# Loads and stores of a graph layer cut into 112 + 13 and 96 + 7 rows, lists issued by another engine, one drain fewer

## Chip, cores and metric

One core of a Trainium2 chip runs the whole program. The metric is the device time of one execution in microseconds. The time shown for a kernel is the median of its runs.

## The reference

One layer of a graph network on 3,125 nodes of 128 features and 53,125 edges of 64 features, all float32. The edges are sorted by their destination `dst`. Cut to what is computed:

```
h   = relu(bn(concat(x[src], edge_attr) @ W1 + b1, g1, be1))   # bn over all edges
s   = segment_sum(h, dst);  cnt = segment_sum(1, dst)
agg = where(cnt > 0, s / max(cnt, 1), 0)
h2  = relu(bn(concat(x, agg) @ W2 + b2, g2, be2))              # bn over all nodes
out = layernorm(x + relu(h2 @ Wl + bl))                        # per node
```

## The kernel before

It is written by hand against the engines: one block of instructions for each engine, ordered as written, with semaphores between them. SyncE (`sp`) issues most DMAs, ScalarE (`act`) some, GpSimd (`pool`) the gathers. A DMA adds 16 to its semaphore when it has landed. There are five stages.

**Start.** `x` lies as 125 partitions of 25 rows. It comes in four loads (`XLOADS`, line 413), is turned by TensorE (line 686, `turn_x`), copied by VectorE (line 992), multiplied by the upper part of W1 (line 702), copied by ScalarE (line 846) and stored as the table `ytab` in DRAM by four stores (`YSAVES`, line 429). W1 is first multiplied by the signs of g1 (lines 984 to 986). The lists `src` and `dst` are loaded as 104 groups of 512 edges, one group to a partition, by `load_lists` (lines 402 and 404): 103 full rows and the remainder in a transfer of its own. VectorE turns them into floats (lines 999, 1000) between its copies of batches 1 and 2, and TensorE spreads them before the last batch. GpSimd starts its gathers when the table has landed (`s_tab`) and the indices stand (`s_idx`).

**Edge loop.** 26 steps of four groups of 512 edges. GpSimd gathers table rows by four indirect DMAs a group (line 606), SyncE loads edge features (`load_ea`, line 435), TensorE turns and multiplies them (716, 722), VectorE adds and sums, ScalarE squares. Three groups of a step stay in SBUF in `res`; the fourth is spilled to DRAM (861). The one-hot matrices go to DRAM too (864), and the products of x with W2 (`h2x_dram`, 877). VectorE adds up the number of edges of each node in `cnt`.

**Spread phase.** 26 steps of four groups. SyncE loads the one-hot matrices back (`load_hot`, 474) and the spilled rows (`load_back`, 484); VectorE takes the maximum (1142), TensorE sums by node in windows of 64 nodes (778), ScalarE copies the window (915), and GpSimd adds it to `agg` (624). On the side the counts go to DRAM (325), VectorE inverts them (`invert_counts`), they go to DRAM once more (329), and from step 10 on they are spread to all partitions of `cnt` by `counts_back` (333), one transfer for every two steps and one for the rest (`last_counts_back`, 337). `load_nodes` (494, 498) and `load_rest` (506, 509) bring `h2x_dram` and x, the latter as 125 partitions of three rows.

**Seam.** When all 104 windows are added, GpSimd drains (line 640) and sets `sums_over`. VectorE (line 1164, two chunks) and GpSimd (line 645, five chunks) multiply `agg` by the reciprocal counts; both wait for `sums_over` and the last of the counts. Before that VectorE scales W2 (line 1158) once all node inputs are there.

**Node phase.** TensorE multiplies the chunks by W2 (822), VectorE adds the part of x (1173), batch statistics follow, then relu, the product with Wl (835), the sum with x and the layer norm; ScalarE writes the normalised rows (line 320). SyncE stores them in seven transfers of 125 partitions by up to four rows (line 569) and waits for them.

```
q.dma_start(cnt[:, bass.ds(k * RCP, RCP)], rc_dram[bass.ds(k * RCP, RCP)].partition_broadcast(P))
pool.wait_ge(agg_added, NG)
pool.drain().then_inc(sums_over, 1)
```

Of the kernel before, what the change touches and what calls it, by code (L numbers as in the profile page):

```python
# [28 lines left out]
I32 = mybir.dt.int32  # L29
# [4 lines left out]
P = 128  # L34
# [3 lines left out]
GROUP = TILES * P  # L38
U = 4
# [6 lines left out]
def gnn_kernel(nc, x, src, dst, ea, W1, b1, g1, be1, W2, b2, g2, be2, Wl, bl, out):  # L46
# [3 lines left out]
    NT = 25  # L50
# [30 lines left out]
    with ctx:  # L81
# [40 lines left out]
        RCP = (N - 1) // RCN // 8 * 8  # L122
        XTP = NT // RCN
        NODEIN = 16 * ((H2 + 1) * (RCN + 1) + 3 + 3 * H2)
        TAB = 16 * (len(YSAVES) + 1)
# [271 lines left out]
        def _(sp):  # L397
            def load_lists():

                sp.wait_ge(s_rowset, 1)  # L400
                for r, d in ((srow, src), (drow, dst)):
                    sp.dma_start(r[0:NG - 1, :].bitcast(I32),
                                  d[0:(NG - 1) * GROUP].rearrange("(g e) -> g e", e=GROUP)).then_inc(s_rows, 16)
                    sp.dma_start(r[NG - 1:NG, 0:LAST].bitcast(I32),  # L404
                                  d[(NG - 1) * GROUP:E].rearrange("(g e) -> g e", g=1)).then_inc(s_rows, 16)
# [16 lines left out]
            yv = ytab[0:N, :].rearrange("(p t) f -> p t f", t=NT)  # L422
# [16 lines left out]
            for q in range(U):  # L439
                load_ea(0, q)  # L440
# [50 lines left out]
            def load_nodes(k, half):  # L491
# [5 lines left out]
                if half == 1:  # L497
                    sp.dma_start(xnv2[:, bass.ds(k * XTP, XTP), :],
# [808 lines left out]
```

## Time and profile before

| | |
|---|---|
| three runs, median | 919.43 us (916.29 to 920.59) |
| the profiled execution | 916.23 us, its span 914.5 us |
| mean granted clock of TensorE | 0.622 |
| busy: TensorE / GpSimd / VectorE / ScalarE | 442.7 / 461.7 / 388.4 / 195.4 us |
| moved by DMA | 83.91 MB, 92 GB/s over the span |

The profile is one execution. Times in it count from the start of the span. A row of the timeline gives the start, the duration, the engine, the line of the kernel, the operation, the tile written and those read, and in brackets how long the engine had been idle and what ended that. SPq and ACTq are the queues that issue DMAs; their durations are those of issuing, not of moving. The DMA share is the mean busy share of the core's 16 DMA engines. No engine is busy for much over half of the span, so the stages have to be read one by one.

### The profile page before, as it was taken

The numbers are of one execution on the slowest core, as the hardware profiler recorded it, in microseconds if no ns is written. First come the engines' busy times: TensorE is split into PE (matmuls) and PEld (weight loads), VectorE is DVE, ScalarE is ACT, GpSimd is POOL, SyncE is SP. The second block draws the span as 40 slices with busy tenths as digits, with TensorE's granted clock in tenths as the row PEclk, the third lists the DMA queues.
The fourth block names the chain that finished last, engine by engine and source line by source line (L and its number), as shares of the span: only waits on it lengthen the run. The fifth ranks groups of instructions, "written<-read, shape, count | busy, mean of one in ns | idle before, by whom it ended". The sixth has DMA issues, their size and how long they took to land.

```text
span 914.5 us, 11316 instructions
## 1 busy us (share of the span) xinstructions
PE 442.7 (48%) x2195; PEld 338.7 (37%) x2195; DVE 388.4 (42%) x801; ACT 195.4 (21%) x517; POOL 461.7 (50%) x572
## 2 busy tenths in 40 slices
PE   1541553443354434335435434544443459998572
PEld 1520332322233322223323222333222239998442
DVE  1331344433334443333444333344333377776385
ACT  0110111111111111111111111111111125645264
POOL 2056655555665555566555556655555623322352
PEclk9955556555555655555655555565555559999777
DMA  1232322323232322233323232333222224777202
GB/s 65 87 92 63 95 87 71 89 80 83 80 93 78 98 71 79 84 80 94 87 71 89 77 86 80 92 89 89 72 78 86 80 92 130 212 224 207 87 1 71
DMA packets 65233, 83.91 MB, mean 92 GB/s; under 512 B 19159, under 2 KB 44168, under 8 KB 65217
## 3 DMA queue, kind: packets, MB, share of 16 engines
q1 hardware_dynamic: 40529, 39.49, 15.2%
q0 software_dynamic: 13312, 27.29, 11.9%
q10 hardware_dynamic: 11376, 16.97, 5.0%
q14 instruction: 12, 0.10, 0.0%
q8 instruction: 4, 0.07, 0.0%
HBM read 63.61 MB, written 20.08 MB: 92 GB/s over the span
## 4 chain that ended last, share of the span: by engine, by line
another core or an unknown queue 45%; PE 22%; issue 9%; DMA 7%; ACT 5%; DVE 4%; ACTq 3%; SPq 3%; POOLq 1%; POOL 0%; DVEq 0%
PE psH L722 12%; DMA res<-spill 4%; PE psH L778 3%; ACT work L854 2%; PE psC L778 2%; PE psT L716 2%; ACT work L868 2%; DMA res<-in_x 2%; SPq L404 2%; ACTq L864 1%; DMA hotb<-hot_dram 1%; PE psH L702 1%; ACTq L877 1%; POOLq L640 1%
## 5 line engine op out<-in xcount | busy, mean ns | idle before, releaser
L722 PE MATMUL psH<-w1e,work 128*128 128x256 f32 x416 | 207.0, 650 | 390.8 <-ACT work L854 284.6
L606 POOL DMA_INDIRECT res<-ytab,srci x312 | 298.9, 958 | 140.9 <-issue 94.8
L722 PEld LDWEIGHTS psH<-w1e,work 128*128 128x128 f32 x416 | 117.6, 312 | 447.4 <-ACT work L854 310.0
L606 POOL DMA_INDIRECT work<-ytab,srci x104 | 100.6, 968 | 193.4 <-DVE res L1044 155.2
L854 ACT ACTIVATE work<-psT 128x256 f32<-128x256 f32 x104 | 40.0, 384 | 571.0 <-remote 417.3
L1058 DVE TENSOR_TENSOR psX<-work,psX 128x512 f32<-128x512 f32 x104 | 72.2, 694 | 120.6 <-issue 60.6
L1044 DVE TENSOR_TENSOR work<-psH,work 128x512 f32<-128x512 f32 x26 | 18.0, 692 | 163.3 <-remote 131.5
L1044 DVE TENSOR_TENSOR res<-psH,res 128x512 f32 (+1 forms) x78 | 54.0, 692 | 69.8 <-PE psH L722 37.2
L1142 DVE TENSOR_TENSOR work<-res,psX 128x512 f32<-128x512 f32 x103 | 70.7, 688 | 28.3 <-PE psC L778 11.5
L716 PE MATMUL psT<-ident,work 128*128 128x128 f32 x208 | 64.7, 411 | 8.9 <-DMA work<-in_edge_attr 7.6
L624 POOL TENSOR_TENSOR agg<-agg,srci 128x64 f32 x104 | 32.2, 309 | 68.1 <-ACT srci L915 66.2
L1038 DVE TENSOR_TENSOR cnt<-cnt,psC 128x64 f32 x104 | 23.1, 222 | 83.3 <-remote 78.5
L778 PE MATMUL psH<-work 128*128 128x128 f32 (+1 forms) x416 | 52.7, 281 | 6.4 <-ACT srci L915 4.8
L732 PEld LDWEIGHTS psC<-hotb,onesb 128*128 128x128 bf16 x416 | 40.5, 137 | 38.2 <-issue 28.6
L1051 DVE TENSOR_TENSOR psS<-res,psS 128x512 f32<-128x512 f32 x78 | 53.8, 690 | 0.0
L778 PEld LDWEIGHTS psH<-work 128*128 128x128 f32 x416 | 50.1, 197 | 7.5 <-ACT srci L915 5.7
L868 ACT ACTIVATE work<-res 128x512 f32 (+1 forms) x78 | 49.0, 628 | 13.9 <-issue 11.2
L778 PE MATMUL psC<-work 128*128 128x128 f32 (+1 forms) x416 | 51.4, 277 | 0.0
L778 PEld LDWEIGHTS psC<-work 128*128 128x128 f32 x416 | 49.3, 194 | 0.0
L1027 DVE TENSOR_TENSOR hotb<-iota,loc 128x256 bf16<-128x256 f32 x104 | 43.3, 416 | 0.0
L732 PE MATMUL psC<-hotb,onesb 128*128 128x64 bf16 x416 | 42.0, 240 | 1.6 <-issue 1.6
L716 PEld LDWEIGHTS psT<-ident,work 128*128 128x128 f32 x208 | 34.4, 210 | 9.3 <-issue 7.8
(146 smaller groups left out, 379.8 us busy)
## 6 DMA issues: line engine op xcount, KB each, us to landing
work<-in_edge_attr SPq DMA_DIRECT2D x103, 128.0 KB
hot_dram<-hotb ACTq DMA_DIRECT2D x26, 256.0 KB
spill<-work ACTq DMA_DIRECT2D x26, 256.0 KB, 2.7
res<-spill SPq DMA_DIRECT2D x25, 256.0 KB, 3.2
res<-ytab,srci POOLq DMA_INDIRECT x312
hotb<-hot_dram SPq DMA_DIRECT2D x13, 256.0 KB, 3.8
work<-hot_dram SPq DMA_DIRECT2D x13, 256.0 KB, 3.5
h2x_dram<-agg ACTq DMA_DIRECT2D x25, 125.0 KB
```

The source lines that it names most:

```text
L606: pool.indirect_dma_start(rows[:, j * F:(j + 1) * F], None, ytab, bass.IndirectOffsetOnAxis(ap=srci[:, j, g:g + 1], axis=0)).then_inc(gath ...
L716: last = pe.transpose(psT[q % 2][:, b * P:(b + 1) * P], ear[:, q % 2, b * P:(b + 1) * P], ident[:, :])
L722: last = pe.matmul(psH[q % 2][:, b * 2 * F:(b + 1) * 2 * F], eat[:, q % 2, b * P:(b + 1) * P], w1e[:, :, :].rearrange("p a f -> p (a f)"), ...
L732: last = pe.matmul(psC[q % 2][:, 0:WIN], onesb[:, :], hotb[:, q, j * WIN:(j + 1) * WIN], start=(j == 0), stop=(j == TILES - 1))
L778: last = pe.matmul(psA[q][:, 0:n], mx[:, q, j * F:(j + 1) * F], hotf[:, q, j * WIN:j * WIN + n], start=(j == 0), stop=(j == TILES - 1))
L854: act.activation(eat[:, q % 2, :], psT[q % 2][:, 0:2 * P], ACT.Copy).then_inc(eat_ready, 1)
L868: act.activation(sq[:, q % 2, :], slot(i, q), ACT.Square).then_inc(sq_ready, 1)
L1027: dve.tensor_tensor(hotb[:, q, :].rearrange("p (j w) -> p j w", j=TILES), iota[:, :].unsqueeze(1).broadcast_to([P, TILES, WIN]), loc[:, :, ...
L1044: dve.tensor_tensor(slot(i, q), psH[q % 2][:, :], slot(i, q), ALU.add).then_inc(h_ready, 1)
L1051: dve.tensor_tensor(psS[:, :], slot(i, q), psS[:, :], ALU.add).then_inc(h_summed, 1)
L1058: dve.tensor_tensor(psX[:, :], sq[:, q % 2, :], psX[:, :], ALU.add).then_inc(sq_summed, 1)
L1142: dve.tensor_tensor(tiles(mx[:, q, :]), tiles(hin), negu, ALU.max).then_inc(m_ready, 1)
```

## The change

- Transfers that have 125 partitions are cut in two by `CUTS`, 112 and 13: the loads of x at the start and before the node phase, the stores of `ytab`, the stores of the output. The list loads of 103 rows are cut in 96 and 7 by `ROWS`. The small transfers of the remainders stay.
- The list loads are issued by ScalarE, behind its two loads of W1 and g1, and no longer by SyncE between the second and the third load of x.
- SyncE issues the first two loads of edge features ahead of the stores of the table instead of behind them.
- The reciprocal counts come back in two transfers of 1,664 and 1,461 nodes, issued when they have landed in DRAM, ahead of step 4 of the spread phase, instead of nine transfers spread over its later steps.
- GpSimd sets `sums_over` by an increment without a drain.

```
-        RCP = (N - 1) // RCN // 8 * 8
+        CUTS = [(0, PN // 16 * 16), (PN // 16 * 16, PN)]
+        ROWS = [(0, (NG - 1) // 16 * 16), ((NG - 1) // 16 * 16, NG - 1)]
...
-        def counts_back(q, k):
-
-            q.dma_start(cnt[:, bass.ds(k * RCP, RCP)], rc_dram[bass.ds(k * RCP, RCP)].partition_broadcast(P)
-                        ).then_inc(s_rcb, 16)
-
-        def last_counts_back(q):
-            q.dma_start(cnt[:, RCN * RCP:N], rc_dram[RCN * RCP:N].partition_broadcast(P)).then_inc(s_rcb, 16)
+        def counts_back(q):
+
+            q.wait_ge(s_rcd, 16)
+            for part in range(2):
+                cut = slice(part * NAGG // 2, min(N, (part + 1) * NAGG // 2))
+                q.dma_start(cnt[:, cut], rc_dram[cut].partition_broadcast(P)).then_inc(s_rcb, 16)
...
-                if k == 2:
-                    load_lists()
-                sp.dma_start(xnv[:, t:t + n, :], xv[:, t:t + n, :]).then_inc(s_x[k], 16)
+                for a, b in CUTS:
+                    sp.dma_start(xnv[a:b, t:t + n, :], xv[a:b, t:t + n, :]).then_inc(s_x[k], 16)
...
+            for q in range(2):
+                load_ea(0, q)
...
-                sp.dma_start(yv[:, t:t + n, :], ysv[:, t:t + n, :]).then_inc(s_tab, 16)
...
+                for a, b in CUTS:
+                    sp.dma_start(yv[a:b, t:t + n, :], ysv[a:b, t:t + n, :]).then_inc(s_tab, 16)
...
-                    sp.dma_start(xnv2[:, bass.ds(k * XTP, XTP), :],
-                                 x[bass.ds(k * XTP * PN, XTP * PN), :].rearrange("(t p) f -> p t f", p=PN)
-                                 ).then_inc(s_nodein, 16)
-                    counts_back(sp, k)
+                    for a, b in CUTS:
+                        sp.dma_start(xnv2[a:b, bass.ds(k * XTP, XTP), :],
+                                     x[bass.ds(k * XTP * PN, XTP * PN), :].rearrange("(t p) f -> p t f", p=PN)[a:b]
+                                     ).then_inc(s_nodein, 16)
...
                 counts_to_dram(sp)
                 load_step(3, 1)
-                sp.wait_ge(s_rcd, 16)
+                counts_back(sp)
...
-                sp.dma_start(ov[:, t:t + n, :], zov[:, t:t + n, :]).then_inc(s_out, 16)
-            sp.wait_ge(s_out, 16 * len(BATCH))
+                for c0, c1 in CUTS:
+                    sp.dma_start(ov[c0:c1, t:t + n, :], zov[c0:c1, t:t + n, :]).then_inc(s_out, 16)
+            sp.wait_ge(s_out, 16 * len(CUTS) * len(BATCH))
...
-                pool.drain().then_inc(sums_over, 1)
+                pool.sem_inc(sums_over, 1)
...
+            act.wait_ge(s_rowset, 1)
+            for r, d in ((srow, src), (drow, dst)):
+                for a, b in ROWS:
+                    act.dma_start(r[a:b, :].bitcast(I32),
+                                  d[a * GROUP:b * GROUP].rearrange("(g e) -> g e", e=GROUP)).then_inc(s_rows, 16)
+                act.dma_start(r[NG - 1:NG, 0:LAST].bitcast(I32),
+                              d[(NG - 1) * GROUP:E].rearrange("(g e) -> g e", g=1)).then_inc(s_rows, 16)
```

The semaphore targets follow the number of transfers. `load_rest` is cut in the same way and loses the last part of the counts.

Two places of the order of instructions. The first is SyncE's at the start, before:

```order
L413 DMA res<-in_x 125x512 x2
L402 DMA res<-in_src 103x512 [waits rows_preset]
L404 DMA res<-in_src 1x389
L402 DMA res<-in_dst 103x512
L404 DMA res<-in_dst 1x389
L413 DMA res<-in_x 125x1024
L413 DMA res<-in_x 125x1152
```

and after the change:

```order
L403 DMA res<-in_x 112x512
L403 DMA res<-in_x 13x512
L403 DMA res<-in_x 112x512
L403 DMA res<-in_x 13x512
L403 DMA res<-in_x 112x1024
L403 DMA res<-in_x 13x1024
L403 DMA res<-in_x 112x1152
L403 DMA res<-in_x 13x1152
```

The four list transfers are gone from this queue, and nothing stands between the loads of x. The second place is ScalarE's beginning after the change; before, its table load followed directly on the first two rows:

```order
L837 DMA w1x<-in_L_gnn_W 128x128
L838 DMA res<-in_L_gnn_g 128x128
L842 DMA res<-in_src 96x512 [waits rows_preset]
L842 DMA res<-in_src 7x512
L844 DMA res<-in_src 1x389
L842 DMA res<-in_dst 96x512
L842 DMA res<-in_dst 7x512
L844 DMA res<-in_dst 1x389
L848 ACT_TABLE_LOAD
L848 ACTIVATE res<-psH 125x512 [waits y_psum] x6
```

Six transfers now stand ahead of the table load and of the first copy of y.

## Rows read from the trace of the kernel before

**Rows 1.** Timeline 0 to 60 us: start, us, engine line operation out<-in, [idle <-releaser]
```profile
9.81 2.24 PE L702 MATMUL psH<-w1x,res 128*125 128x128 f32 x8 [0.17 <-DVE res L992]
...
26.93 0.43 DVE L999 CAST res<-res 104x512 f32<-104x512 int32 x1 [16.15 <-DMA res<-in_dst]
...
31.64 2.06 PE L702 MATMUL psH<-w1x,res 128*125 128x128 f32 x8
...
44.47 0.28 ACT L846 ACTIVATE res<-psH 125x128 f32<-125x128 f32 x1 [1.00 <-PE psH L702]
...
51.86 1.17 POOL L606 DMA_INDIRECT res<-ytab,srci  x1 [46.09 <-DMA ytab<-res]
```

**Rows 2.** The chain that ended last, start of the program: start us, us, what
```profile
16.56 14.15 DMA res<-in_x
...
36.71 1.87 PE psH L702 x8
...
39.00 1.86 PE psH L702 x8
```

**Rows 3.** Timeline of SyncE's DMA issues at the start
```profile
2.08 6.16 SPq L404 DMA_DIRECT2D res<-in_src  x1
...
8.60 7.91 SPq L404 DMA_DIRECT2D res<-in_dst  x1
...
44.77 0.26 SPq L429 DMA_DIRECT2D ytab<-res  x1
```

**Rows 4.** Stretches: length us, granted clock, DMA share of 16 engines, GB/s
```profile
12.00:14.00 2.00, 1.00 0.06 25
795.00:800.00 5.00, 1.00 0.97 278
908.00:910.00 2.00, 0.50 0.36 109
```

**Rows 5.** Stretches of the spread phase: us, busy per engine (x), clock, DMA share, GB/s
```profile
766.30:787.70 21.40, 21.40 (x194) 21.40 (x194) 16.48 (x24) 13.03 (x48) 7.41 (x24) 1.00 0.53 159
787.70:848.40 60.70, 55.78 (x490) 54.99 (x490) 42.02 (x63) 31.87 (x123) 18.66 (x61) 1.00 0.76 227
```

**Rows 6.** The page's DMA issues: count, KB each, us from issue to landing
```profile
spill<-work ACTq DMA_DIRECT2D x26, 256.0 KB, 2.7
res<-spill SPq DMA_DIRECT2D x25, 256.0 KB, 3.2
```

**Rows 7.** Timeline around the seam
```profile
855.46 0.35 DVE L1158 TENSOR_SCALAR res<-res,col 128x256 f32<-128x256 f32 x1 [2.48 <-DMA res<-in_x]
...
864.97 2.31 DVE L1164 TENSOR_TENSOR agg<-agg,cnt 128x500 f32<-128x500 f32 x2 [9.16 <-POOLq L640]
...
865.70 3.70 PE L822 MATMUL psT<-agg,res 128*128 128x500 f32 x4 [9.23 <-DVE agg L1164]
...
872.87 1.84 PE L822 MATMUL psC<-agg,res 128*128 128x500 f32 x4
```

**Rows 8.** Line 640, GpSimd's drain: duration ns min/median/max, first and last start us
```profile
L640 POOLq DRAIN  x1: 8568/8568/8568, 856.4 to 856.4; - x1
```

**Rows 9.** Stretches at the seam
```profile
858.00:871.40 13.40, 5.70 (x7) 2.52 (x8) 4.55 (x6) 1.24 (x4) 5.93 (x6) 0.50 0.00 1
856.70:864.70 8.00, 0.00 (x0) 0.00 (x0) 0.00 (x0) 0.00 (x0) 0.00 (x0) 0.57 0.00 0
```

**Rows 10.** Timeline at the end, ScalarE and SyncE's queue
```profile
904.77 1.64 ACT L320 ACTIVATE res<-res 125x128 f32<-125x128 f32 x4
...
908.33 2.20 SPq L569 DMA_DIRECT2D out_dram<-res  x1
```

**Rows 11.** SyncE's waits: us in total, times, longest
```profile
SPq L81 <- DMA out_dram<-res: 3.6, 1, 3.6
```

**Rows 12.** The chain at the beginning of the spread phase
```profile
754.00 3.67 PE psH L778 x16
```

**Rows 13.** The page's costliest groups: busy us, mean ns | idle before, releaser
```profile
L606 POOL DMA_INDIRECT work<-ytab,srci x104 | 100.6, 968 | 193.4 <-DVE res L1044 155.2
```

More of the change, by code:

```diff
@@ L121, in gnn_kernel @@
         RCN = NI // 2 - 5
-        RCP = (N - 1) // RCN // 8 * 8
         XTP = NT // RCN
-        NODEIN = 16 * ((H2 + 1) * (RCN + 1) + 3 + 3 * H2)
-        TAB = 16 * (len(YSAVES) + 1)
+        CUTS = [(0, PN // 16 * 16), (PN // 16 * 16, PN)]
+        ROWS = [(0, (NG - 1) // 16 * 16), ((NG - 1) // 16 * 16, NG - 1)]
+        NODEIN = 16 * ((H2 + len(CUTS)) * (RCN + 1) + 3 + 3 * H2)
+        TAB = 16 * (len(CUTS) * len(YSAVES) + 1)
         ghot = work2[:, :, :].rearrange("p q w -> p (q w)")
@@ L397, in _ @@
         def _(sp):
[L398 to L405, printed above, removed]
             xv = x.rearrange("(p t) f -> p t f", t=NT)
@@ L421, in _, with load_ea @@
             sp.dma_start(ytab[N:YROWS, :], zeros[0:YROWS - N, :]).then_inc(s_tab, 16)
+            def load_ea(i, q):
+                if not first(i, q, 2):
+                    sp.wait_ge(ea_turned, U * i + q - 1)
+                s = ea_loaded[q % 2]
+                sp.dma_start(ear[:, q % 2, :],
+                             ea[bass.ds((i * U + q) * GROUP, GROUP), :].rearrange(
+                                 "(p j) f -> p (j f)", j=TILES)).then_inc(s, 16)
+            for q in range(2):
+                load_ea(0, q)
             yv = ytab[0:N, :].rearrange("(p t) f -> p t f", t=NT)
@@ L428, in _ @@
                 sp.wait_ge(s_ysb, done)
-                sp.dma_start(yv[:, t:t + n, :], ysv[:, t:t + n, :]).then_inc(s_tab, 16)
-            def load_ea(i, q):
-                if not first(i, q, 2):
-                    sp.wait_ge(ea_turned, U * i + q - 1)
-                s = ea_loaded[q % 2]
-                sp.dma_start(ear[:, q % 2, :],
-                             ea[bass.ds((i * U + q) * GROUP, GROUP), :].rearrange(
-                                 "(p j) f -> p (j f)", j=TILES)).then_inc(s, 16)
-            for q in range(U):
+                for a, b in CUTS:
+                    sp.dma_start(yv[a:b, t:t + n, :], ysv[a:b, t:t + n, :]).then_inc(s_tab, 16)
+            for q in range(2, U):
                 load_ea(0, q)
@@ L508, in load_rest @@
                                  ).then_inc(s_nodein, 16)
-                sp.dma_start(xnv2[:, RCN * XTP:NT, :],
-                             x[RCN * XTP * PN:N, :].rearrange("(t p) f -> p t f", p=PN)).then_inc(s_nodein, 16)
+                for a, b in CUTS:
+                    sp.dma_start(xnv2[a:b, RCN * XTP:NT, :],
+                                 x[RCN * XTP * PN:N, :].rearrange("(t p) f -> p t f", p=PN)[a:b]).then_inc(s_nodein, 16)
             def load_weights():
@@ L555, in _ @@
                 counts_to_dram(sp)
-                sp.wait_ge(s_rcd, 16)
+                counts_back(sp)
                 with sp.Fori(0, RCN) as k:
@@ L681, in turn_x @@
                 t0, n = BATCH[b]
-                pe.wait_ge(s_x[next(k for k, part in enumerate(XLOADS) if BATCH[b] in part)], 16)
+                pe.wait_ge(s_x[next(k for k, part in enumerate(XLOADS) if BATCH[b] in part)], 16 * len(CUTS))
                 if b >= 2:
@@ L996, in _ @@
             turned_x(1)
-            dve.wait_ge(s_rows, 64)
+            dve.wait_ge(s_rows, 96)
             dve.tensor_copy(srowf[0:NG, :], srow[0:NG, :].bitcast(I32))
@@ L1159, in _ @@
             dve.wait_ge(sums_over, 1)
-            dve.wait_ge(s_rcb, 16 * (RCN + 1))
+            dve.wait_ge(s_rcb, 32)
             for c0, cw in CHUNKS[:DVE_MEAN]:
```

3 lines of the change are left out of this document (1 added, 2 removed).

## The prediction

> **What bounds the kernel now.** I read the page's head first, then the start of the program in order of time, then the granted bandwidth in three stretches, then the spread phase, the seam and the end. The profiled execution has a span of 914.5 us and took 916.23 us; the three runs have a median of 919.43, so this execution lies 3.2 us below it. Everything below is summed against the 916.23 us and then carried to the median.
>
> The span falls into five stages. The start, until the first gather at 51.86 us [rows 1], fills the node table. The edge loop from there to about 745 us is set by gathers of 64 KB that GpSimd issues, 416 of them at just under 1 us each, 104 of these after a wait for the one buffer that is spilled [rows 13]; no edit touches it, and I cost it at nothing. The spread phase follows to 856.3, then the seam, then the node phase and the writing of the output.
>
> The start is a transfer problem. SyncE needed 6.16 and 7.91 us to issue two list remainders of 1.5 KB, because the 103-row transfers ahead of them had filled something that the queue must wait for [rows 3]. While those ran alone, all 16 engines together were busy 0.06 of the time and moved 25 GB/s: one engine of sixteen. A stretch in which nothing runs but output in 125 rows shows 0.36 and 109 GB/s. A stretch with 128-row transfers mixed in reaches 0.97 and 278 GB/s [rows 4]. So here the rows of a transfer set how many engines carry it. The third load of x, issued at 16.56, let TensorE go on 14.15 us later, at 30.71 [rows 2], and VectorE could turn the destination list into floats only from 26.93. From there the compute chain (transposes, products, copies) runs with little idle to the last copy of y at 44.47 + 0.28; the gathers still wait until 51.86 for the last piece of the table to land [rows 1].
>
> **The change, part by part.**
>
> Lists on ScalarE and split rows, start. The first products still start at 9.81, behind VectorE's copy [rows 1], which itself stands behind the signs for W1; the change leaves these loads as they are. After that the second batch follows when TensorE is free: two batches lie 39.00 - 36.71 = 2.3 us apart in the chain [rows 2], so batch 1 starts near 12.0 instead of 31.64. From batch 1 to the end of the last copy took 44.75 - 31.64 = 13.1 us, lists included, so that copy ends at 25.1: **-19.6 us**. The two list casts, 0.43 us each, were done while TensorE waited [rows 1] and now stand between the copies of batches 1 and 2; VectorE's own copies leave about half of each 2.3 free, so they are covered. What must be true is that x and both lists have landed by about 12 us. By their shapes they are 1,562 and 412 KB; with the weights 2.3 MB. At the 227 GB/s of the spread phase [rows 5] that is 10.1 us, from 1.5 to 11.6; at 278 GB/s 8.3 us. That is just in time, and a late last list costs 1 us or two. SyncE now issues 8 loads where it had 4, at some 0.26 us each when nothing blocks [rows 3], 2 to 3 us in all, and ScalarE 6 at the same price ahead of its table load, while its first copy comes only at 12: covered, both.
>
> Last piece of the table. It was issued at 44.77 and landed at 51.86, 7.1 us, behind 0.5 MB pieces in 125 rows [rows 1, 3]. Now two issues of 0.26 us, then a landing. The nearest row is the spill, 256 KB in 128 rows, 2.7 us [rows 6]. 7.1 - 3.3: **-3.8 us**. The first two edge loads now go ahead of the table, which costs SyncE two issues where it waits for y anyway; that they used to come late was no term of its own beside the gathers.
>
> Together the start gives -23.4. No row shows a transfer of 112 or 96 rows. From below it is bounded by the 125-row case (nothing gained but SyncE's blocking), from above by the 128-row case. I take the upper one, since both 128 and 112 are many times 16 while 125 and 103 are not, and the rows of [rows 4] rank exactly so.
>
> Here the Trainium skill decides for the same side: "DMA: Bandwidth & Descriptors", section "Why a DMA increments its semaphore by 16 and not by 1", says that a transfer runs on the largest number of engines up to 16 that divides its outermost size on both sides. By that rule 103 rows run on 1 engine, 125 on 5, 112 and 96 on 16, 13 on 13 and 7 on 7. The trace agrees for 103 (0.06) and roughly for 125 (0.36, where 5 of 16 would be 0.31).
>
> Spread phase. A step issues one reload of spilled rows, which I counted. The six steps between 766.3 and 787.7 took 21.4 / 6 = 3.57 us each with TensorE busy all the time; the 15 steps to 848.4, in which x, h2x and the counts are loaded too, took 60.7 us, 4.05 each [rows 5]. Loss by transfers: 60.7 - 15 x 3.57 = 7.2 us. The change takes the counts' nine loads out of it and lets x use all engines. I let three quarters go: -5.4. SyncE's issues are even: one more for x, one less for counts, per pair of steps. Against it stand the counts, 128 x 3,125 x 4 bytes = 1.6 MB issued at once near 764, in front of the next reload of spilled rows. At 227 GB/s they take 7.0 us; at 278 GB/s 5.8. A reload normally takes 3.2 us to land [rows 6] and has room for about as much again, so I charge 3.0 for one stall, bounds 0 and 7.0. **-2.4 us** net, bounds +7.0 and -7.2.
>
> Seam. GpSimd's drain starts at 856.4 behind its last addition and takes 8.57 us [rows 8]; no engine and no transfer runs in these 8 us [rows 9], and VectorE starts at 864.97 [rows 7]. A semaphore increment in its place leaves about 0.1: **-8.5 us**. Next late would be the node inputs: VectorE scaled W2 at 855.46, after the last x had landed [rows 7]. Without the drain that leaves about 1 us; SyncE's last issues come about half a microsecond earlier and land faster, so I cost that at nothing. If the cover is gone it costs the excess alone.
>
> The clock behind the seam. From 858 to 871.4 TensorE was granted 0.50, 1.2 GHz, after it had gone idle at the seam [rows 9]; its first four half products took 3.70 us, the same four 1.84 later at 2.4 GHz [rows 7]. Without idle time it keeps the upper level, which saves 1.9 us on the first four and half as much on the next two, of which VectorE's own work hides a little: **-2.3 us**, bounds 0 and -2.8.
>
> End. ScalarE finishes at 906.41, but SyncE issues the last 62.5 KB only at 908.33, takes 2.20 us for it, held up as in the start [rows 10], and then waits 3.6 us for the landing, to 914.1 [rows 11]. Now: two issues to 907.1, landing 2.7 at most [rows 6], 909.8; before it landed at 914.1. **-4.3 us**, bounds 0 and -5.5.
>
> Sum: -19.6 - 3.8 - 2.4 - 8.5 - 2.3 - 4.3 = -40.9 us. 916.23 - 40.9 = 875.3 for an execution like the profiled one; against the median of 919.43 it is **878.5 us**.
>
> **The rivals.**
>
> 1. The drain is not the cause (7 in 100). What GpSimd does in those 8.57 us may have to be done whatever stands there, and its next instruction then waits. For it: 8.57 us [rows 8] is much for a flush when nothing is under way. Against: the profile shows nothing that it would be doing. Both the seam and the clock term go: 878.5 + 10.8 = 889.3.
>
> 2. Pieces in series (6 in 100). Three times a wait now ends with two transfers in place of one: first x, last y, last output. If the second piece costs a whole landing each time, it is 3 x 2.7 = 8.1 [rows 6]: 886.6. Against it: issues are 0.3 us apart and overlap in the profile. The Trainium skill's rule on "Two transfers to disjoint partition halves" (same page, "Rules for kernel authors") says that they serialize on the same engines and one of 128 partitions is better; no run here shows this yet, and it takes the whole to be on 16 engines, which [rows 4] deny for 125 rows.
>
> 3. The counts in one burst (6 in 100). They stall the reload for their full 7.0, the contention stays, and the pause lowers the clock for a stretch as behind the seam, where it was low for 13.4 us or more [rows 9], half of them lost. +4.0 + 5.4 + 6.8: 894.7. Against it: with 8% of idle time the clock stayed at 1.00 [rows 5].
>
> 4. The split does nothing (2 in 100): 112 rows go as 125 did. Then the seam and its clock alone remain: 919.4 - 10.8 = 908.6.
>
> 5. Slower (2 in 100). The spread phase runs at 1.2 GHz. At the lower level two groups took 3.67 us [rows 12], at the upper one 3.57 / 2 = 1.79 [rows 5]; for the 52 pairs of groups this costs up to 52 x 1.88 = 98 us. The stalls of the burst would have to keep TensorE down for 41 / 98, over 42% of the phase, before the change turns into a loss; in full it would be 976. The clock was at 1.00 through the phase, idle shares of 8% included, which speaks against it.
>
> **How the numbers follow.** My own case has 77 in 100, and within it the start may give 19 to 26 and the spread phase +2 to -7: 870 to 886. The range of 8 in 10 is 869 to 890 and takes in the drain rival and the pieces; the burst, the split without effect and the slower case lie outside. A measurement of this kernel can tell about 0.5%, 4.6 us, from no change. Faster by more than that: all but rival 5 and a little, 0.97; within: 0.01; slower: 0.02.
>
> **What would show it.** The first gather near 28 us; list remainders issued in 0.3 us; DMA busy over 0.6 of the 16 engines between 3 and 9 us. Reloads every 3.57 us nearly up to the seam, one longer gap near 767. VectorE's first mean 0.2 us after GpSimd's last addition, the first four half products at under 2 us. The last output landing 3.5 us after ScalarE's end. The prediction is wrong if x still lands after 15 us, if the seam still stands idle for over 2 us, or if the steps of the edge loop are not 26.7 us any more.

## Result and profile after the change

The changed kernel takes 879.16 us in the median of four runs (878.30 to 882.68), the kernel before 918.61 in four runs of the same comparison (the three runs shown ahead and one more). The ratio is 0.958, with a 95% interval of 0.954 to 0.961: 4.2% faster, where 878.5 was predicted. Where the executions of a kernel fall into a fast and a slow group, a ratio is formed from the fast ones alone, so it is not always the quotient of the medians shown. The profiled execution took 878.30 us, its span is 876.0 us and TensorE's mean granted clock 0.618; before it was 916.23, 914.5 and 0.622.

| stage, from the two profiled executions, us | before | after | difference | predicted |
|---|---|---|---|---|
| start of the span to the first gather | 51.86 | 27.37 | -24.5 | -23.4 |
| first gather to the last | 686.75 | 688.27 | +1.5 | 0 |
| last gather to the first window added | 18.07 | 18.00 | -0.1 | 0 |
| first window added to the last (spread phase) | 99.66 | 97.40 | -2.3 | -2.4 |
| last window to VectorE's mean (seam) | 8.63 | 0.08 | -8.55 | -8.5 |
| VectorE's mean to ScalarE's end | 41.44 | 41.56 | +0.1 | -2.3 |
| ScalarE's end to the end of the span | 8.08 | 3.30 | -4.8 | -4.3 |
| sum | 914.49 | 875.98 | -38.5 | -40.9 |

**The start.** The timeline of the changed kernel (columns as in [rows 1, 3]), first ScalarE's and SyncE's issues, then what waited for them:

```profile
0.79 3.47 SPq L403 DMA_DIRECT2D res<-in_x  x8
...
2.85 0.24 ACTq L844 DMA_DIRECT2D res<-in_src  x1
...
3.86 0.29 ACTq L844 DMA_DIRECT2D res<-in_dst  x1
...
11.18 1.09 PE L681 MATMUL psC<-ident,res 125*128 125x125 f32 x4 [0.22 <-DMA res<-in_x]
...
12.06 0.43 DVE L1001 CAST res<-res 104x512 f32<-104x512 int32 x1 [1.80 <-DMA res<-in_dst]
...
24.51 0.28 ACT L848 ACTIVATE res<-psH 125x128 f32<-125x128 f32 x1 [1.00 <-PE psH L697]
...
27.37 1.17 POOL L601 DMA_INDIRECT res<-ytab,srci  x1 [21.60 <-DMA ytab<-res]
```

The remainders of the lists, which took SyncE 6.16 and 7.91 us [rows 3], are issued in 0.24 and 0.29; eight loads of x take 3.47. The last copy of y ends at 24.79 instead of 44.75, the first gather starts 2.58 us after it instead of 7.11. Two stretches and two more that are used below (length, busy of PE, PEld, DVE, ACT, GpSimd with counts, clock, DMA share, GB/s):

```profile
3.00:9.00 6.00, 2.05 (x9) 1.69 (x10) 1.72 (x4) 1.28 (x1) 2.77 (x1) 1.00 0.90 219
...
768.50:822.20 53.70, 53.70 (x483) 53.70 (x483) 41.38 (x61) 32.81 (x120) 18.47 (x60) 1.00 0.79 227
...
834.00:845.00 11.00, 8.62 (x24) 4.02 (x22) 10.90 (x23) 8.18 (x27) 11.00 (x23) 1.00 0.00 1
845.00:856.00 11.00, 4.46 (x23) 4.49 (x24) 9.78 (x24) 5.54 (x11) 3.25 (x8) 0.53 0.00 0
```

Between 3 and 9 us the engines are busy 0.90 and move 219 GB/s; lists in one piece gave 0.06 and 25 [rows 4].

**The spread phase.** TensorE's timeline has one pause, where a reload of spilled rows stands behind the two transfers of counts (832 and 730.5 KB, landed 6.4 and 7.4 us after their issue):

```profile
745.92 1.95 PE L773 MATMUL psC<-work 128*128 128x128 f32 x16
750.02 3.44 PE L773 MATMUL psH<-work 128*128 128x128 f32 x16 [2.15 <-ACT srci L917]
```

VectorE's row at the same place names what came last:

```profile
750.09 0.69 DVE L1144 TENSOR_TENSOR work<-res,psX 128x512 f32<-128x512 f32 x1 [2.27 <-DMA res<-spill]
```

The pause itself is 2.2 us, and the two groups behind it run at the lower clock, 3.44 us where 1.95 stood before: 1.5 more. Together some 3.8, where 3.0 was charged. Behind it TensorE is busy in 53.70 of 53.70 us, while the transfers keep the DMA engines busy 0.79: every step takes 3.57 us. Before, the same steps were stretched. Two groups of products that lie 15 steps apart in the kernel before:

```profile
788.52 1.95 PE L778 MATMUL psH<-work 128*128 128x128 f32 x16
...
848.24 1.99 PE L778 MATMUL psH<-work 128*128 128x128 f32 x16
```

These 15 steps took 59.7 us, and 15 undisturbed ones take 53.6. The contention was 6.1 us, and all of it came back, not three quarters. The 7.2 us of the prediction are 1 us too much: its stretch of 60.7 us [rows 5] holds 490 products, at 32 a step 15.3 steps and not 15.

**The seam and what follows.** The timeline there:

```profile
827.76 0.35 DVE L1160 TENSOR_SCALAR res<-res,col 128x256 f32<-128x256 f32 x1
...
830.72 0.32 POOL L619 TENSOR_TENSOR agg<-agg,srci 128x64 f32 x1 [0.60 <-ACT srci L917]
831.12 2.32 DVE L1166 TENSOR_TENSOR agg<-agg,cnt 128x500 f32<-128x500 f32 x2 [3.00 <-POOLq L635]
...
831.85 1.94 PE L817 MATMUL psT<-agg,res 128*128 128x500 f32 x4 [1.17 <-DVE agg L1166]
```

VectorE's mean starts 0.08 us after the last addition has ended, W2 was ready 3 us ahead, and the first four half products take 1.94 us instead of 3.70 [rows 7]. VectorE's last reduction of the batch statistics starts 14.20 us after the mean (16.91 before, 881.88 - 864.97). Then a row that was harmless before becomes long:

```profile
845.32 0.17 DVE L1183 TENSOR_REDUCE res<-res 128x2 f32<-128x14 f32 x1 [0.42 <-ACT res L946]
845.52 2.75 DVE L1184 TENSOR_SCALAR res<-res 128x2 f32<-128x2 f32 x1
```

Two numbers per partition take 2.75 us; the same instruction took 0.17 before, as its neighbours do. It ends at 848.27. GpSimd's timeline says why that moment:

```profile
837.84 10.40 POOL L647 TENSOR_TENSOR res<-res 125x128 f32<-125x128 f32 x25
```

25 additions of `bl` to x end at 848.24. In the kernel before the two rows read

```profile
871.69 10.44 POOL L652 TENSOR_TENSOR res<-res 125x128 f32<-125x128 f32 x25
...
882.08 0.17 DVE L1182 TENSOR_SCALAR res<-res 128x2 f32<-128x2 f32 x1
```

There the instruction came when the additions were as good as over. GpSimd has this work from the seam on, 17.1 us in either kernel, and as soon as TensorE is faster, VectorE waits for it.

**The end.** ScalarE ends at 871.05 + 1.63 = 872.68, SyncE waits 1.1 us for the output where it waited 3.6 [rows 11], and the span ends at 875.98. But GpSimd's own last instruction in the program, a drain that is part of every program, reads (duration ns min/median/max, start):

```profile
L81 POOLq DRAIN  x1: 9722/9722/9722, 866.0 to 866.0; - x1
```

It ends at 875.74, some 0.4 us after SyncE's wait for the output is over (874.21 + 1.1), and the last semaphores of the program follow it. So it decides the end, but only by some 0.2 us: the kernels below in which this drain is short end 3.05 to 3.13 us after ScalarE, those with the long one 3.29 to 3.30 (where the output is cut). In the kernel before it took 1.20 us. The difference is 8.5 us, the price of the drain that was taken out of the seam.

### The profile page after: what moved, and what is told of

It reads as the page before. It is cut to its first block, busy times and chain, and to the rows that moved or that the text cites. A ratio compares the mean times of both kernels' runs of the same rounds, so it can differ in the third digit from the quotient of the medians.

```text
span 876.0 us, 11335 instructions
## 1 busy us (share of the span) xinstructions
PE 439.6 (50%) x2195; PEld 338.6 (39%) x2195; DVE 390.4 (45%) x801; ACT 196.4 (22%) x517; POOL 459.2 (52%) x572
## 4 chain that ended last, share of the span: by engine, by line
another core or an unknown queue 47%; PE 25%; issue 11%; ACT 6%; DVE 5%; ACTq 3%; DMA 2%; SPq 0%; POOL 0%; DVEq 0%; POOLq 0%
PE psH L717 11%; PE psH L773 5%; PE psC L773 5%; ACT work L856 2%; ACT work L870 2%; PE psT L711 1%; ACTq L866 1%; ACTq L879 1%; PE psH L697 1%; DMA res<-in_x 1%; DVE res L1175 1%; DMA hotb<-hot_dram 1%; ACT agg L877 1%; DMA work<-ytab 1%
```

## Experiments

The theory after the first reading: A, the number of rows alone, and what divides it, decides how many engines carry a transfer; B, GpSimd's drain pays once for the gathers, wherever the first one stands; C, the clock behind the seam was really gained and eaten by GpSimd's 25 additions; D, the burst of counts costs one pause and sometimes a stretch of lower clock. Rivals were that the queue, not the cut, cured the start; that any drain costs 8.57 us; that the two small pieces cost a landing each; and that the time lost behind the seam is TensorE's.

The runs of this section come from three chips. On each the kernel before was run beside: 910.18 us (seven runs), 916.13 (seven) and 905.93 (eleven). The edge loop alone takes 680.5 to 682 us on the first and third and 687 to 688 on the second, so times are compared through the ratio or on one chip. The changed kernel's ratio of 0.958 gives 871.9 on the first chip and 877.6 on the second; these are worked out, not run, and by the interval of the ratio good to some 3.3 us either way.

**Two drains in place of the increment.**

```
-                pool.sem_inc(sums_over, 1)
+                pool.drain()
+                pool.drain().then_inc(sums_over, 1)
```

> The changed kernel with two GpSimd drains, one directly behind the other, where it has the increment. Theory A, a drain has a price of its own whether or not anything is under way: both take about 8.6 us, VectorE's first mean starts 17 us later, the time is 879 + 17 = 896 us. Theory B, the drain waits once for something that GpSimd still has open: the first takes about 8.6, the second under 0.5, and the time rises by about 8.6 to 888. Either way the clock behind the seam falls to 1.2 GHz. If GpSimd's 25 additions, and not the clock, bound the first half of the node phase, the rise of the time is the rise of the seam alone and VectorE's first tensor_scalar behind the statistics takes 0.2 us again instead of 2.75; if the clock is worth 2.3 us there, the rise is 2.3 us more than the seam's.

Measured: 881.43 us (877.76 to 884.12), ratio 0.970 [0.966, 0.973], 9.5 us above the 871.9. The drains of this kernel, at the seam and at the program's end:

```profile
L635 POOLq DRAIN  x1: 8568/8568/8568, 822.5 to 822.5; - x1
```

```profile
L636 POOLq DRAIN  x1: 40/40/40, 831.1 to 831.1; - x1
```

```profile
L81 POOLq DRAIN  x1: 1192/1192/1192, 866.3 to 866.3; - x1
```

The first one costs the 8,568 ns of the kernel before [rows 8], to the nanosecond; the second 40 ns; the one at the end is back to 1.2 us. The price is paid once, by the first drain. The time rose by 9.5 us, as for one drain, and not by 17. Its place also tests C. TensorE went idle and to a clock of 0.51 (826 to 836 us), and the reduction came 15.92 us after the mean, 1.7 later than in the changed kernel; yet from the mean to ScalarE's end it took 41.77 us, against 41.56. The late reduction merely waited less for GpSimd:

```profile
847.09 0.17 DVE L1184 TENSOR_REDUCE res<-res 128x2 f32<-128x14 f32 x1 [0.41 <-ACT res L947]
847.29 1.03 DVE L1185 TENSOR_SCALAR res<-res 128x2 f32<-128x2 f32 x1
```

**The lists uncut, on ScalarE.**

```
-        ROWS = [(0, (NG - 1) // 16 * 16), ((NG - 1) // 16 * 16, NG - 1)]
+        ROWS = [(0, NG - 1)]
```

> The changed kernel with the lists still issued by ScalarE but as 103 rows and not as 96 + 7. Theory, the row count sets the engines: 2 x 206 KB go through one engine at 25 GB/s, 16.5 us, with that engine's share of x behind or between; VectorE turns the destination list only at 19 to 22 us instead of 12.1, the first gather is at 35 to 37 instead of 27.4, the time 887 to 889. Rival, the gain of the start lies in taking the lists off SyncE's queue: the first gather stays within 1 us of 27.4 and the time at 879.

Measured: 891.16 us (888.49 to 894.45), ratio 0.981 [0.977, 0.984], 19 us above the 871.9. The timeline at the start:

```profile
2.34 5.84 ACTq L844 DMA_DIRECT2D res<-in_src  x1
...
8.79 11.99 ACTq L844 DMA_DIRECT2D res<-in_dst  x1
...
20.80 1.28 ACT L848 ACT_TABLE_LOAD   x1 [20.80 <-issue]
...
31.07 0.43 DVE L1001 CAST res<-res 104x512 f32<-104x512 int32 x1 [17.97 <-DMA res<-in_dst]
...
46.55 1.17 POOL L601 DMA_INDIRECT res<-ytab,srci  x1 [40.78 <-DMA ytab<-res]
```

The blocked issue moved to ScalarE's queue with the lists and grew. The first gather comes 19.2 us later than in the changed kernel, some 10 more than was expected. What decides is the destination list: it is there at 31.07, 19.0 us later than in the changed kernel and later even than in the kernel before (26.93), and VectorE, which makes TensorE's next input behind it, waits 17.97 us for it. Its load could be issued only when the source list's blocked issue was over, at 8.2. ScalarE's table load and first copies also stand behind the blocked issues, until 20.8, but they are done by 23.2 and hold nothing up. That the cut is needed is shown; the estimate had the list there at 19 to 22.

**The cut lists, on SyncE**, where they stood before.

```
                t, n = part[0][0], sum(w for _, w in part)
+                if k == 2:
+                    sp.wait_ge(s_rowset, 1)
+                    for r, d in ((srow, src), (drow, dst)):
+                        for a, b in ROWS:
...
```

> The changed kernel with the lists cut in 96 + 7 but issued by SyncE between the second and the third load of x, as before. Theory, the row count did it: six issues of 0.3 us put the third load of x 2 us later, the transfers are bound by their volume anyway, first gather 27 to 29, time 878 to 881. Rival, the queue did it: SyncE blocks again for several us at the list remainders and the first gather comes at 35 or later, time 887.

Measured: 869.91 us (868.39 to 871.16), ratio 0.956 [0.953, 0.960], not to be told from the changed kernel's. The timeline:

```profile
3.28 0.27 SPq L408 DMA_DIRECT2D res<-in_src  x1
...
4.33 0.25 SPq L408 DMA_DIRECT2D res<-in_dst  x1
...
26.32 1.17 POOL L609 DMA_INDIRECT res<-ytab,srci  x1 [20.55 <-DMA ytab<-res]
```

With cut lists nothing blocks on SyncE either. The move to ScalarE is worth nothing by itself; the 96 + 7 rows did it.

**x as 124 + 1 rows at the start**, the lists cut as in the change. Both have two pieces; only the size of the first differs.

```
+        XCUTS = [(0, PN - 1), (PN - 1, PN)]
...
-                for a, b in CUTS:
+                for a, b in XCUTS:
                     sp.dma_start(xnv[a:b, t:t + n, :], xv[a:b, t:t + n, :]).then_inc(s_x[k], 16)
```

> The changed kernel with the four loads of x at the start cut as 124 + 1 rows and not as 112 + 13. Theory, the largest divisor up to 16 of the row count sets the engines: 124 = 4 x 31 has 4, one fewer than 125 uncut, so the 16 engines' share falls from 0.90 to about 0.5 between 3 and 9 us, the third and fourth load land 2 to 6 us later, the first gather is at 30 to 33, the time 881 to 885. Rival, what counts is being near 128 rows, or having two transfers in flight: first gather within 0.5 of 27.4, share as in the changed kernel.

Measured: 881.49 us (880.38 to 883.21), ratio 0.969 [0.965, 0.973], 9.6 us above the 871.9. The stretch of 3 to 9 us, then TensorE's waits for x in the timeline:

```profile
3.00:9.00 6.00, 1.07 (x4) 0.71 (x4) 1.50 (x4) 1.28 (x1) 2.77 (x1) 1.00 0.43 144
```

```profile
6.71 1.07 PE L682 MATMUL psC<-ident,res 125*128 125x125 f32 x4 [6.71 <-DMA res<-in_x]
11.38 1.09 PE L682 MATMUL psC<-ident,res 125*128 125x125 f32 x4 [3.60 <-DMA res<-in_x]
16.40 1.09 PE L682 MATMUL psC<-ident,res 125*128 125x125 f32 x4 [2.09 <-DMA res<-in_x]
```

The share falls from 0.90 to 0.43 for a change of 12 rows, and the eight issues take 6.61 us instead of 3.47. The first gather is at 36.05, later than the 30 to 33 expected: the last copy of y ends 6.4 us later, and the last piece of the table, cut as in the change, still lands 4.9 us behind it instead of 2.6, for which no row gives the reason. So it is not the number of rows as such (124 is close to 128) and not the pair of pieces, but what divides the rows. The Trainium skill's rule (DMA: Bandwidth & Descriptors, Why a DMA increments its semaphore by 16 and not by 1) gives 4 engines for 124 and 16 for 112; the two measured shares rank as it says.

**Node inputs and outputs uncut, the start cut.**

```
+        WHOLE = [(0, PN)]
...
-                for c0, c1 in CUTS:
+                for c0, c1 in WHOLE:
                     sp.dma_start(ov[c0:c1, t:t + n, :], zov[c0:c1, t:t + n, :]).then_inc(s_out, 16)
```

> The changed kernel with the loads of x before the node phase and the stores of the output uncut, 125 rows; start and table stay cut. Theory, 125 rows run on 5 engines: in the spread phase these engines are near full in the stretch where x and h2x are loaded, so a step takes 3.7 to 3.9 us there instead of 3.58 (the counts are gone, so less than the 4.05 of before), 2 to 5 us in all; at the end the last issue is held up again and the program ends 8 us after ScalarE's last row instead of 3.3, +4.8. Sum +7 to +10 against the changed kernel. Rival for the spread phase: the counts alone made the contention, steps stay at 3.58 and the sum is +4.8.

Measured: 881.98 us (879.40 to 883.80), ratio 0.964 [0.960, 0.967], 4.4 above the 877.6. From ScalarE's end to the end of the span it took 8.14 us, against 3.30; SyncE's wait for the output reads

```profile
SPq L81 <- DMA out_dram<-res: 3.5, 1, 3.5
```

as before the change [rows 11], so the whole output term, 4.8 us, belongs to the cut. The 7 to 10 us expected did not come, for in the spread phase the uncut x costs little: 96.62 us, against 94.6 to 96.1 in the other kernels with the burst whose clock held. The 16 steps from the first window of the tenth to the first of the last, 514 or 515 products, first in the kernel before, then here, then in the changed kernel (columns as in the stretches above):

```profile
790.00:853.30 63.30, 58.38 (x514) 57.59 (x513) 43.77 (x64) 33.33 (x129) 19.78 (x64) 1.00 0.75 223
...
767.20:824.90 57.70, 57.43 (x515) 57.30 (x514) 43.58 (x64) 34.55 (x129) 19.71 (x65) 1.00 0.78 219
...
770.90:828.00 57.10, 57.10 (x514) 57.10 (x513) 43.97 (x65) 34.87 (x129) 19.67 (x64) 1.00 0.77 223
```

x in 125 rows without the counts beside it costs 0.6 us, not 6.2.

**Counts not in one burst**, in two ways: one transfer in each later pair of steps as before, with the rest of the change kept, and six small ones spread over steps 4 to 9.

```
-                counts_back(sp)
+                sp.wait_ge(s_rcd, 16)
...
+                    counts_back(sp, k)
```

> The changed kernel with the reciprocal counts brought back in eight transfers of 192 KB and a rest, spread over steps 10 to 25 as before. Theory: the stall of 3.8 us near step 4 (2.3 us of idle TensorE and 1.5 of low clock) goes, the steps from 10 on take 3.6 to 3.75 us instead of 3.58 because x no longer crowds five engines, +0.3 to +2.5; spread phase 1.3 to 3.5 us shorter than in the changed kernel. Rival, the counts were the contention: steps at 4.0 us, +6.5 and -3.8, 2.7 longer.

```
                         load_step(2 * k + par, par)
+                        counts_part(sp, k, par)
+                counts_rest(sp)
```

> The changed kernel with the reciprocal counts brought back in six transfers of 520 nodes (260 KB), one behind each of the steps 4 to 9, and a rest of 5 nodes. In these steps the DMA engines are half idle. Theory: the stall near step 4 goes and nothing takes its place, the clock stays at 2.4 GHz through the phase, the spread phase is 3.8 us shorter. Rival, each piece delays the reload behind it by a microsecond and the stall is spread out: 0 to -1.

Measured: 876.69 us (875.65 to 878.43), ratio 0.958 [0.955, 0.961], and 877.34 (874.69 to 877.78), 0.958 [0.955, 0.961]. Both equal the changed kernel's ratio, 0.958. In the profile of the first

```profile
736.00:765.00 29.00, 29.00 (x261) 29.00 (x260) 22.30 (x35) 17.36 (x65) 9.84 (x33) 1.00 0.49 139
```

shows no pause and no fall of the clock, and the spread phase took 95.17 and 95.69 us against 97.40. That is a gain of about 2 us over this one execution, not over the burst as such: seven other profiles with the burst, in which the clock held, lie at 94.6 to 96.6. The six small transfers, from which 3.8 us were expected, met one pause later on:

```profile
770.25 1.99 PE L784 MATMUL psH<-work 128*128 128x128 f32 x16 [1.62 <-ACT srci L928]
```

The late counts stand beside a cut x here, and the same 16 steps read

```profile
766.70:825.00 58.30, 57.62 (x514) 57.35 (x514) 43.29 (x64) 34.24 (x129) 19.70 (x65) 1.00 0.84 241
```

The counts without an uncut x beside them cost 1.2 us (2.0 in the last kernel of this section, which has them late too), an uncut x without the counts 0.6, and both together 6.2 in the kernel before. So neither made the contention by itself, and either change alone takes most of it away. With x cut, the burst saves 1.2 us in the late steps and pays for it with a pause of TensorE of 1.2 to 3.4 us; it was not needed.

**GpSimd's 25 additions as seven**, one for each batch.

```
-            for t in range(NT):
-                rows = xn[0:PN, t * F:(t + 1) * F]
-                last = pool.tensor_tensor(rows, rows, blr[0:PN, :], ALU.add)
+            for t, n in BATCH:
+                rows = xn[0:PN, t * F:(t + n) * F].rearrange("p (t f) -> p t f", t=n)
+                last = pool.tensor_tensor(rows, rows, blr[0:PN, :].unsqueeze(1).broadcast_to([PN, n, F]), ALU.add)
```

> The changed kernel with GpSimd's 25 additions of bl to rows of x (0.42 us each, 10.5 us) made as seven of up to four tiles at once (about 1.1 us each, some 7.2 us). Theory: VectorE's first tensor_scalar behind the batch statistics took 2.75 us instead of 0.17 because it can't run while GpSimd works through its additions, and ended with them; GpSimd now ends 3.3 us earlier, before VectorE comes there, the instruction takes 0.17 again, and from the seam to ScalarE's last row it takes 39.0 us instead of 41.6. Rival, the 2.75 us are not GpSimd's doing (a late statistic, an instruction fetch): they stay. The program's end: GpSimd's own drain there took 9.72 us and ended 0.2 us before the end, now it starts with the last sum 2.6 us earlier too, so the end follows by 2.6.

Measured: 875.32 us (872.38 to 877.85), ratio 0.955 [0.951, 0.959]. The timeline:

```profile
839.05 7.84 POOL L647 TENSOR_TENSOR res<-res 125x512 f32<-125x512 f32 x7
...
846.50 0.17 DVE L1183 TENSOR_REDUCE res<-res 128x2 f32<-128x14 f32 x1 [0.41 <-ACT res L946]
846.70 0.21 DVE L1184 TENSOR_SCALAR res<-res 128x2 f32<-128x2 f32 x1
```

GpSimd is done 14.6 us after the mean instead of 17.1, the short instruction, which comes 0.2 us before that, takes 0.21 us, and from the mean to ScalarE's end it is 39.30 us: 2.3 less than in the changed kernel and 2.1 less than in the kernel before, where the prediction had booked 2.3 for the clock. C holds. The Trainium skill (SBUF — State Buffer, Who interferes with whom) says that VectorE in a two-port mode and GpSimd exclude each other from a shared pair of ports, each for one instruction. The row agrees in who waits; but it waited 2.75 us, over six additions of 0.42 us (10.40 / 25), not one, and in which mode the instruction ran no row says. The median lies 2.3 below the 877.6 of this chip, less than what the times can tell; it is the stage that shows the gain. In the profiled execution the gain does not show, for its spread phase took 99.92 us; behind the burst the clock was low for 7 us:

```profile
749.00:756.00 7.00, 6.34 (x30) 6.34 (x31) 2.75 (x4) 2.83 (x11) 1.55 (x5) 0.51 0.40 121
```

**The changed kernel again**, on the third chip, so that the following runs have it beside them.

> The changed kernel once more, unedited, as the base for the other three on the same chip. Ratio to the kernel before 0.954 to 0.961. What its profile should tell beside: the spread phase takes 95 to 96 us if the clock holds through the burst of counts and 97 to 100 if it falls, the rest agrees within 1 us with the first profile.

Measured: 872.78 us (868.06 to 874.80, six runs), ratio 0.968 [0.961, 0.975], above the 0.954 to 0.961 expected. The interval is wide because the kernel before ran from 891.88 to 910.57 on this chip. Here the profiled execution shows the burst's pause without a fall of the clock: 22.62 of 25 us busy, clock 1.00, the phase 96.09 us.

```profile
740.00:765.00 25.00, 22.62 (x202) 22.62 (x203) 17.19 (x25) 14.31 (x54) 8.02 (x26) 1.00 0.62 175
```

Over all ten profiles that had the burst, the clock fell at the pause in three, for 3.4 to 6.9 us: at pauses of 2.15, 2.82 and 3.43 us. At the other seven pauses, 1.21 to 2.77 us long, it held. The three took 97.40, 98.21 and 99.92 us for the phase, the other seven 94.6 to 96.6.

**The last edge load, 97 rows, as 96 + 1.**

```
-            sp.dma_start(ear[0:LP, 1, :],
-                         ea[e0:e0 + LP * TILES, :].rearrange("(p j) f -> p (j f)", j=TILES)).then_inc(s, 16)
+            for a, b in ((0, LP // 16 * 16), (LP // 16 * 16, LP)):
+                sp.dma_start(ear[a:b, 1, :],
+                             ea[e0 + a * TILES:e0 + b * TILES, :].rearrange("(p j) f -> p (j f)", j=TILES)).then_inc(s, 16)
```

> The changed kernel with the 97 rows of edge features of the last group cut as 96 + 1. 97 has no divisor up to 16 but 1, and the changed kernel's chain shows 6.0 us for this load. Theory: it lands 3 to 3.5 us earlier, TensorE's last product is no longer the last, and the wait passes to the gather of the last group, whose rows land about 3 us after its issue: from the last gather to GpSimd's first window addition it takes 15.0 to 15.6 us instead of 18.0. Rival, the gather is last anyway: 17.5 to 18.

Measured: 867.84 us (866.49 to 877.65), ratio 0.966 [0.955, 0.977]; no difference that can be told. From the last gather to the first window it took 16.78 us instead of 17.52, where 15.0 to 15.6 was expected. The miss has a reason in the timeline: TensorE's groups follow each other every 3.24 us up to the end, so the late load was hidden but for 0.7 us.

```profile
706.69 2.07 PE L718 MATMUL psH<-w1e,work 128*128 128x256 f32 x4 [0.47 <-ACT work L857]
...
709.93 2.07 PE L718 MATMUL psH<-w1e,work 128*128 128x256 f32 x4 [0.47 <-ACT work L857]
```

**A drain right behind the last gather**, where GpSimd has nothing else to do for 13 us.

```
                     gather(i, q)
+            pool.drain()
```

> The changed kernel with a GpSimd drain directly behind its last gather, where GpSimd then waits 13 us for VectorE. Theory, the first drain behind the gathers pays 8.57 us once, wherever it stands: this one takes 8.6 us and is hidden, the drain at the program's end takes 1.2 us instead of 9.72, and the end, which followed that drain by 0.3 us, now follows the landing of the output: 0.2 to 0.4 us earlier, not to be told from zero in the times. Rival, the price comes with GpSimd's own additions: the early drain is short and the last one takes 9.7 us still.

Measured: 870.86 us (869.68 to 874.91), ratio 0.968 [0.958, 0.977]. The drain is recorded from 706.9 on for 12.15 us, beside the last gathers, and ends at 719.03, 8.6 us after the last of them; GpSimd's next work, at 723.78, waits for VectorE. The one at the program's end is short again:

```profile
L81 POOLq DRAIN  x1: 1210/1210/1210, 857.9 to 857.9; - x1
```

B holds at a third place. A drain ahead of all gathers, which every kernel has behind GpSimd's first memsets, ends 0.06 us after the memset in front of it, so the price was not there yet. The tail became 3.13 us instead of 3.30: since the output lands at nearly the same time, little was to be had.

**Four edits together**: the counts late, the seven additions, the 96 + 1 rows and the early drain, each as shown above.

> The changed kernel with the counts spread over steps 10 to 25, GpSimd's additions of bl in seven instructions, the last group's load as 96 + 1 and the early drain. Theory, the gains add: 2 to 4 us in the spread phase and its clock, 2.3 in the node phase, 2.5 to 3 before the spread phase, 0.3 at the end: 7 to 9.5 us below the changed kernel on the same chip, ratio to the kernel before 0.948 to 0.952. Rival, a hidden wait takes one of them (GpSimd's drain reaching into VectorE's marks, or the last gather): 4 to 6 us.

Measured: 864.21 us (863.52 to 865.10, six runs), ratio 0.958 [0.952, 0.965]. On the same chip the changed kernel has 872.78, and no run of the one lies within the range of the other: 8.6 us less. Stage by stage the two profiled executions (865.10 and 868.95 us) differ by less: 1.0 us to the first window, 0.4 in the spread phase, 2.4 behind the mean (39.50 against 41.89), 0.25 in the tail. The short instruction is short in this kernel too:

```profile
835.00 0.17 DVE L1190 TENSOR_REDUCE res<-res 128x2 f32<-128x14 f32 x1 [0.41 <-ACT res L953]
835.20 0.20 DVE L1191 TENSOR_SCALAR res<-res 128x2 f32<-128x2 f32 x1
```

The rest of the 8.6 us lies in executions that were not profiled: the changed kernel scatters over 6.7 us, this one over 1.6. 8.6 - 3.9 = 4.7 us are left. The burst, whose pause sometimes takes the clock down, could do that: it is the one disturbance of varying price that was seen, and its dearest case lay 4.4 us above the middle of the seven others (99.92 against 95.5). But the kernel before has no burst and scatters over 18.7 us on this chip. It is not shown that the unprofiled executions were such cases, and this stays open.

## Why the prediction was right, and where it was not

The forecast of 878.5 us met 879.16, and that it came so near is in part luck. For an execution like the profiled one it was 875.3, and 878.30 came: 3.0 us off. The stages miss by 2.4 together: 2.4 us too much was forecast for the clock and 1.5 for the edge loop, 1.1 too little at the start and 0.5 at the end; the rest lies outside the span. Carried to the medians the miss shrank to 0.7, because the profiled execution before lay 2.4 us below its median (3.2 when the forecast was made) and the one after only 0.9.

- **Lists and x, -19.6**: the last copy of y came 19.96 us earlier. The reason given, divisors and not the engine that issues, is shown by the lists left whole (+19 us), by the same cut lists on SyncE (no loss) and by 124 + 1 rows (+9.6). The two losses overlap and do not add up. Rival 4, a split that does nothing, is out.
- **Last piece of the table, -3.8**: measured -4.5, 2.58 us from the last copy to the gather. How much of it is the cut, and how much that edge loads no longer follow the last piece at once, as they did at 45.08, no run separates.
- **Spread phase, -5.4 + 3.0**: net measured -2.3, but the two terms were each 0.7 to 0.8 too small and cancelled. The contention was 6.1 us and not 7.2, by the misread stretch, and all of it came back and not three quarters: it took the late counts and the uncut x together (6.2 us; 1.2 and 0.6 by themselves), and the change removes both. The burst cost 3.8 in this execution, of which 1.5 is clock. Rival 3 named the mechanism, pause and then lower clock, correctly; its price of 16 us was far too high, because the pause was 2.2 us and not 7.0 and the clock was low for 3.4 us and not 13.4.
- **Seam, -8.5**: measured -8.55. Rival 1 was half right. What the drain does has to be done: it reappears at the end, 9.72 us long. But no later work of GpSimd had to wait for it, and at the end it runs beside the tail and outlasts SyncE's wait for the output by 0.4 us, which costs some 0.2. Had SyncE's last output landed any sooner, nothing would have been gained by it.
- **The clock behind the seam, -2.3**: this is the step that failed. The half products ran at 1.94 us as said and the statistics came 2.7 us earlier; from the mean to ScalarE's end the measured gain is -0.1, that is none. The prediction looked only at TensorE and VectorE there and did not ask what GpSimd was doing in these 17 us. The run with seven additions is 2.3 us shorter there than the changed kernel and 2.1 shorter than the kernel before: the size was right, and VectorE's wait for GpSimd, which ate it, was missed.
- **End, -4.3**: measured -4.8, and 4.8 given back by the uncut output. Rival 2, pieces in series, would have cost 2.7 us at each of three places; the last two pieces are landed 3.3 us after ScalarE's end, and the first gather comes 2.6 us after its last copy. Out.
- **The edge loop, 0**: +1.5 us in 687. No edit explains it, and between chips the same loop differs by 7; it is taken for scatter between executions. The step of 26.7 us did not change.
- **Rival 5**, the phase at the lower clock: the clock was at 1.00 in nearly all of it.

## What to carry to other kernels

Look at the number of rows of each transfer, and where it is not a multiple of 16 (103, 124, 125 here) cut off the largest multiple: the remainder costs an issue of 0.3 us, and the cuts gave most of the 24 us at the start and 5 at the end. When two loads slow each other down, find out whether taking away one of them is enough before changing both. When an engine on the path becomes faster, look at what the others do beside it, down to instructions of 0.2 us that never mattered. A wait that is moved to where nobody needs it is as good as one removed, but only as long as it stays shorter than what hides it.

## What the runs showed of the hardware

- After a program's gathers, GpSimd's first drain costs some 8.5 us more than the next one (8,568 ns, then 40), at the seam, at the program's end (9.72 against 1.20) or right behind the gathers (ending 8.6 us after the last). What it does in that time no row shows.
- A VectorE instruction on 128x2 numbers took up to 2.8 us and ended 0.02 to 0.03 us after GpSimd's back-to-back additions were over, while VectorE's additions, statistics and reductions beside them ran on at their usual durations. It ended so in all thirteen profiles of changed kernels, and took 2.75 to 2.79 us in the ten in which it came that long before the additions' end, and 1.03, 0.21 and 0.20 in the three in which it came later.
- A transfer of 103 rows, which keeps one DMA engine's worth busy (0.06 of 16), blocks the queue on which the next one is issued: 6.16 and 7.91 us on SyncE before, 5.84 and 11.99 on ScalarE with uncut lists.
- A pause of TensorE of 1.2 to 3.4 us in the busy spread phase brought the lower clock in three of ten profiled executions, at 2.15, 2.82 and 3.43 us, and not in the other seven, one of them 2.77 us long; what decides between them was not found.
- Loads of x in 125 rows (0.6 us) and of the counts (1.2 us) hardly slow TensorE's steps by themselves; together they cost 6.2 us in the same 16 steps.
